# Preparing the last layer's weights inside the first attention, and eight tiles in a written-out order

## The reference

```
x = x + tanh(g_xattn[0]) * attention0(layernorm(x), ctx)   # 32 query heads, 8 kv heads, dim 128, rope, wo
x = x + tanh(g_ffn[0])   * ffn0(layernorm(x))              # weights faked to 4 bits, activations to 8 bits, silu(gate)*up, 512-1376-512
x = x + tanh(g_xattn[1]) * attention1(layernorm(x), ctx)   # channels as tokens: 512 x 512 logits per sequence, q and k from ctx
x = x + tanh(g_ffn[1])   * ffn1(layernorm(x))              # dense 512x512 + bias + 4 LoRA experts of rank 8, softmax router
```

## Time and profile before

| | us |
|---|---|
| median of three runs | 862.97 |
| the profiled execution | 863.2 |
| its span, first to last instruction | 861.2 |
| PE / DVE / ACT / POOL busy in the span | 817.4 / 573.4 / 457.7 / 495.6 |

### The profile page before, as it was taken

One profiled execution on the slowest core, in us unless ns is written; L12 is line 12 of the kernel. 1 busy time (PEld: TensorE's weight loads), 2 busy tenths in 40 slices (PEclk: granted clock), 3 DMA queues, 4 the chain that ended last, 5 costly groups with the idle time before them and its releaser, 6 DMA issues. The chain is left out here.

```text
span 861.2 us, 13801 instructions
## 1 busy us (share of the span) xinstructions
PE 817.4 (95%) x5025; PEld 652.8 (76%) x5025; DVE 573.4 (67%) x1057; ACT 457.7 (53%) x864; POOL 495.6 (58%) x424
## 2 busy tenths in 40 slices
PE   5999999999999999999999999997759999999996
PEld 5778888888888888888888888886526777777774
DVE  4977765656755565565655446446588999999863
ACT  3544555545554444543545434331468878887760
POOL 1767556654566655666457655451247867776750
PEclk9999999999999999999999999999789999999998
DMA  8522132331423313132130130074133333222300
GB/s 258 135 87 80 56 93 59 104 97 38 117 59 87 93 29 93 38 110 70 28 117 25 41 26 2 1 232 133 49 98 75 87 87 98 57 66 64 74 14 25
DMA packets 74499, 66.77 MB, mean 78 GB/s; under 512 B 36112, under 2 KB 53744, under 8 KB 74048
## 3 DMA queue, kind: packets, MB, share of 16 engines
q1 hardware_dynamic: 73472, 65.56, 27.8%
q10 hardware_dynamic: 960, 0.33, 0.1%
HBM read 49.04 MB, written 6.34 MB: 64 GB/s over the span
## 5 line engine op out<-in xcount | busy, mean ns | idle before, releaser
L791 DVE SCALAR_TENSOR_TENSOR x_res<-bank,gate,x_res 128x512 f32<-128x512 f32 x128 | 95.6, 748 | 96.2 <-PE bank L485 95.8
L963 POOL TENSOR_TENSOR prob<-prob,row_inv 128x512 f32<-128x512 f32 x32 | 33.4, 1044 | 191.4 <-DVE row_inv L787 191.4
L949 POOL TENSOR_TENSOR rope_swap<-rope_swap,trig 128x512 f32<-128x512 f32 x80 | 103.9, 1299 | 33.7 <-ACT rope_swap L609 33.6
L78 PE MATMUL bank<-xnT_hi,wq_hi 128*128 128x512 f32 (+1 forms) x264 | 105.4, 399 | 0.7 <-DVE xnT_lo L726 0.7
L480 PE MATMUL bank<-wo_hi,oT_hi 128*128 128x512 f32 x256 | 101.3, 396 | 3.8 <-DVE x_res L791 1.4
L80 PE MATMUL bank<-xnT_hi,wq_lo 128*128 128x512 f32 (+1 forms) x264 | 103.0, 390 | 0.0
L79 PE MATMUL bank<-xnT_lo,wq_hi 128*128 128x512 f32 (+1 forms) x264 | 102.4, 388 | 0.0
L481 PE MATMUL bank<-wo_lo,oT_hi 128*128 128x512 f32 x256 | 101.1, 395 | 0.0
L762 DVE TENSOR_TENSOR rope_cos<-bank,trig 128x512 f32<-128x512 f32 x80 | 54.6, 682 | 69.3 <-PE bank L80 69.3
L608 ACT COPY rope_swap<-bank 64x512 f32<-64x512 f32 x80 | 46.7, 583 | 87.3 <-DVE rope_cos L762 84.4
L1982 POOL TENSOR_TENSOR b_e<-b_e,b_inv 128x512 f32<-128x512 f32 x64 | 69.6, 1091 | 30.2 <-DVE b_inv L1546 29.5
(11 more groups left out here) (228 smaller groups left out, 1960.3 us busy)
## 6 DMA issues: line engine op xcount, KB each, us to landing
wq_raw<-in_L_xattn_wq SPq DMA_DIRECT2D x16, 512.0 KB, 4.1
wo_raw<-in_L_xattn_wo SPq DMA_DIRECT2D x16, 512.0 KB, 3.9
xn<-in_L_ffn_Wd SPq DMA_DIRECT2D x16, 256.0 KB, 3.3
b_ctx<-in_ctx SPq DMA_DIRECT2D x32, 128.0 KB, 2.6
b_k_twice<-b_qk_hi SPq DMA_DIRECT2D x32, 128.0 KB, 2.3
w_T_dram<-w_out SPq DMA_DIRECT2D x28, 128.0 KB, 2.3
w_T<-w_T_dram SPq DMA_DIRECT2D x2, 1376.0 KB, 7.0
xn<-in_L_ffn_Wg SPq DMA_DIRECT2D x10, 256.0 KB, 3.9
```

Of the source, the lines that this page charges most:

```text
L78: pe.matmul(out, a_hi, b_hi, start=first, stop=False)
L791: dve.scalar_tensor_tensor(out=K.x[:, t, :], in0=wo_ps[t % 2][:, :], scalar=K.gate[:, 0:1], in1=K.x[:, t, :], op0=ALU.mult, op1=ALU.add).t ...
L949: pool.tensor_tensor(out=sw, in0=sw, in1=sin_b, op=ALU.mult).then_inc(s_rope, 1)
```

## The change

**Moved into slots 30 and 31 of the attention part:** the selection of experts (DVE, in slot 30 between the first and second, and the second and third accumulate), two `iota` and two `memset` (POOL, at the start of slot 30), `qkv_T` and `base_T(0)` (PE, end of slot 30), `base_T(1)`, `base_T(2)` (slot 31, ahead of the product with v), `base_T(3)` and `b_T` ahead of the last output, `low_T` in the middle of it, `low_b_select` and the first tile's `x_transpose` behind it; with them the copies on ACT, differences on DVE, the statistics of the first four tiles and the first tile's `front`, `x_shifted`, `x_int` and `xT_copy`.

**Loads:** W_base is loaded as soon as the last wq piece is split, the other raw weights ahead of the quantised FFN weights; lora_B comes in 4 DMAs of 128x16x8 elements instead of 16 of 128x4x8; the first tile's context is loaded before the attention part ends.

**Moved between engines, for every tile:** `normalise` of attention1's input goes from DVE to ACT (with a new small `shift_of` on DVE), `x3_lo` from DVE to POOL. `route_end` loses one DVE operation (alpha and z in one). `low` has 132 columns instead of 36.

**Order:** the loops over `it` are replaced on all engines by lists of calls, with explicit waits. Buffers are laid over those of the attention part that are already free.

```diff
+            for par in range(2):
+                sp.wait_ge(s_wq_lo[par], NQP * HKV)
+            load_base(sp, R1, K.a)
             sp.wait_ge(s_proj, NI * (HKV - 1) + pos_of(HKV - 1, "v", 1) + 1)
+            load_block1(sp, K.W1, R1, K.a)
             for w in range(2):
                 sp.dma_start(K.W.T[w][:, :, :], K.T_dram[w]).then_inc(K.s_w_in, 16)
...
-            load_block1(sp, K.W1, K.raw1, K.a)
...
-            load_base(sp, K.raw1, K.a)
+            sp.wait_ge(s_wo, UT * (2 * NPAIR - 2))
+            for par in range(2):
+                load_context(sp, M, ctx_dram, 0, par)
...
+                if U == 2 * NPAIR - 1:
+                    base_T(1)
+                    base_T(2)
...
+                if U == 2 * NPAIR - 2:
+                    qkv_T()
+                    base_T(0)
 
             run_slots(slot)
-            output(2 * NPAIR - 1)
+            base_T(3)
+            b_T()
+            output(2 * NPAIR - 1, low_T)
+            low_b_select()
+            first_x_transpose()
...
+            def selection_of_experts():
+                dve.wait_ge(R1.s_in, 16 * R1.n_loads)
+                dve.wait_ge(s_zero, 2)
+                dve.tensor_copy(M.act_f[:, :], R1.act_i[:, :]).then_inc(s_sel, 1)
+                dve.tensor_copy(M.rank_f[:, :], M.rank_i[:, :]).then_inc(s_sel, 1)
...
                         accumulate(T, T % NT)
+                    if U == 2 * NPAIR - 1:
+                        statistics(k)
+                    if U == 2 * NPAIR - 2 and k == 0:
+                        selection_of_experts()
+                    if U == 2 * NPAIR - 2 and k == 1:
+                        selection_matrices()
...
+            base_low_part(2)
+            last = UT * (2 * NPAIR - 1)
+            accumulate(last, UT)
+            dve.wait_ge(s_x_stat, 2 * UT + 2)
+            front_tile(dve, K, M, 0)
+            accumulate(last + 1, UT + 1)
+            base_low_part(3)
+            for tl in range(2, UT):
+                accumulate(last + tl, UT + tl)
+            low_b_lo()
...
+                    if U == 2 * NPAIR - 2:
+                        pool.iota(M.rank_i[:, :], pattern=[[1, RANK]], base=0, channel_multiplier=0).then_inc(s_zero, 1)
+                        pool.iota(M.part_i[:, :], pattern=[[0, 1]], base=0, channel_multiplier=1).then_inc(s_zero, 1)
...
-    for e in range(E_ALL):
-        load(R.b[:, :, e * RANK:(e + 1) * RANK], a["L1_ffn_lora_B"][e].rearrange("(c p) r -> p c r", p=P))
+    for c in range(DC):
+        load(R.b[:, c, :].rearrange("p (e r) -> p e r", e=E_ALL),
+             a["L1_ffn_lora_B"][:, c * P:(c + 1) * P, :].rearrange("e p r -> p e r"))
...
-            for it in range(NT + 4):
-                if ok(it - 3):
-                    attend_pair(it - 3, 0)
...
+            gate_mm(0, 0)
+            up_mm(0, 0)
+            qk(0, 0)
+            pe.wait_ge(s_gate, 1)
+            gate_mm(0, 1)
```

More of the change, by code:

```diff
@@ new lines, in _ @@
+            logits(2, 2)
+            pe.wait_ge(s_xT_sb, 4)
+            v_item(1)
+            low(0)
+            weights_T(1, 6)
+            pe.wait_ge(s_gate, 10)
+            gate_mm(3, 1)
+            pe.wait_ge(s_v, 2)
+            qk(3, 1)
+            logits(2, 3)
+            weights_T(1, 7)
+            logits(2, 4)
+            pe.wait_ge(s_gate, 11)
+            gate_mm(3, 2)
+            pe.wait_ge(s_up, 10)
+            up_mm(3, 1)
+            attend_pair(1, 0)
+            weights_T(2, 0)
@@ new lines, in _ @@
+            weights_T(3, 5)
+            x3_T(2)
+            pe.wait_ge(s_hTa_sb, 5)
+            down(4)
+            weights_T(3, 6)
+            pe.wait_ge(s_qk_lo[1], 6)
+            v_item(3)
+            logits(4, 2)
+            pe.wait_ge(s_up, 17)
+            up_mm(5, 2)
+            logits(4, 3)
+            low(2)
+            weights_T(3, 7)
+            pe.wait_ge(s_v, 4)
+            x_transpose(6)
+            pe.wait_ge(s_out, 5)
+            gate_mm(5, 2)
+            attend_pair(3, 0)
@@ new lines, in _ @@
+            h_scales(0)
+            scale_gate(1, 0)
+            row_max(0, 4)
+            scale_up(1, 0)
+            reciprocal(0, 1)
+            lo_qk(1, 0)
+            scale_gate(1, 1)
+            row_max(0, 5)
+            row_max(0, 6)
+            make_h(1, 0)
+            scale_up(1, 1)
+            reciprocal(0, 2)
+            front(2)
+            scale_gate(1, 2)
+            row_max(0, 7)
+            scale_up(1, 2)
+            make_h(1, 1)
+            lo_qk(2, 0)
+            output(0)
@@ new lines, in _ @@
+            rest_of_weights()
+            row_max(1, 0)
+            reciprocal(0, 3)
+            statistics(0)
+            scale_gate(2, 0)
+            lo_qk(2, 1)
+            shift_of(0)
+            row_max(1, 1)
+            make_h(1, 2)
+            row_max(1, 2)
+            reciprocal(1, 0)
+            h_scales(1)
+            row_max(1, 3)
+            scale_up(2, 0)
+            front(3)
+            reciprocal(1, 1)
+            scale_gate(2, 1)
+            row_max(1, 4)
+            residual(0)
@@ new lines, in _ @@
+            make_h(2, 0)
+            x3_normalise(0)
+            row_max(1, 5)
+            lo_qk(3, 0)
+            output(1)
+            row_max(1, 6)
+            scale_up(2, 1)
+            reciprocal(1, 2)
+            scale_gate(2, 2)
+            statistics(1)
+            scale_up(2, 2)
+            row_max(1, 7)
+            row_max(2, 0)
+            shift_of(1)
+            make_h(2, 1)
+            reciprocal(1, 3)
+            scale_gate(3, 0)
+            row_max(2, 1)
+            make_h(2, 2)
@@ new lines, in _ @@
+            output(2)
+            row_max(2, 6)
+            make_h(3, 1)
+            row_max(2, 7)
+            scale_gate(4, 0)
+            statistics(2)
+            lo_qk(4, 0)
+            scale_up(4, 0)
+            shift_of(2)
+            zT_lo(0)
+            row_max(3, 0)
+            reciprocal(2, 3)
+            make_h(3, 2)
+            row_max(3, 1)
+            lo_qk(4, 1)
+            h_scales(3)
+            scale_gate(4, 1)
+            reciprocal(3, 0)
+            residual(1)
@@ new lines, in _ @@
+            scale_gate(5, 0)
+            reciprocal(3, 2)
+            lo_qk(5, 0)
+            zT_lo(1)
+            residual(2)
+            statistics(3)
+            scale_up(5, 0)
+            scale_gate(5, 1)
+            x3_normalise(2)
+            finish(1)
+            shift_of(3)
+            reciprocal(3, 3)
+            row_max(4, 0)
+            row_max(4, 1)
+            lo_qk(5, 1)
+            scale_up(5, 1)
+            front(6)
+            reciprocal(4, 0)
+            output(4)
@@ new lines, in _ @@
+            make_h(5, 0)
+            row_max(4, 2)
+            row_max(4, 3)
+            statistics(4)
+            scale_gate(5, 2)
+            route(2)
+            make_h(5, 1)
+            scale_up(5, 2)
+            reciprocal(4, 1)
+            row_max(4, 4)
+            shift_of(4)
+            route_end(2)
+            row_max(4, 5)
+            front(7)
+            scale_gate(6, 0)
+            reciprocal(4, 2)
+            row_max(4, 6)
+            lo_qk(6, 1)
+            row_max(4, 7)
@@ L1756, in _ @@
+            finish(6)
+            route(7)
+            route_end(7)
+            zT_lo(7)
+            finish(7)
         @block.scalar
```

1860 lines of the change are left out of this document (1304 added, 556 removed).

## The result

| | before | after |
|---|---|---|
| median, us | 863.12 (862.83 to 864.4, 4 runs) | 852.25 (849.12 to 856.15, 4 runs) |
| ratio, 95% interval | | 0.9873 (0.9831 to 0.9916) |
| profiled execution / its span | 863.2 / 861.2 | 856.15 / 854.3 |
| measured again, the kernel before beside it | 862.02 (17 runs) | 850.54 (847.73 to 856.11, 6 runs), ratio 0.9870 (0.9840 to 0.9900) |

The change makes the kernel faster by 1.3%, some 11 us. The forecast was 848.0, range 835 to 861. The profiled execution of the kernel after is the slowest of its four; of the repetition there is a profile of the fastest (847.73, span 845.8). The two together tell what varies.

The account below looks back on a forecast made before the run. Tail taken as bound by latency at start and end, by DVE with PE close behind in the middle; from 863.2, -2.2 - 5.9 - 2.6 - 1.0 - 3.0 - 0.3 = -15.0 gives 848.2, forecast 848, range 835 to 861.

Parts of the forecast that it names:

- B: Rival: weight preparation not hidden, lora_B late, clock low through the last output, no steady gain; 857 us, chance 0.19.
- C: Rival: slower, x3_lo waits at the head of POOL's list and delays weigh and product every tile; 866 us, chance 0.08.
- A: Rival: relief worth more, 1.0 us a tile for seven tiles, end gives 5, clock stays up; 839 us, chance 0.28.
- Preparation out of the tail, -9.5: Between last output and first gate: weight preparation moves ahead, so gate_mm could start at 608.1 instead of 617.6, -9.5 us.
- The selection's stall, +4.3: Slot 30: second accumulate waits for the selection, which waits for POOL's iotas; PE stands still 4.3 us, delaying what follows.
- The clock, +3: Attention's end: the new pause puts PE at 1.2 GHz for some 4 us, +2; low_T before 512-column matmuls, +1 (0 to 3).
- wrong if the first gate lies before 611: Sign against the forecast: a first gate matmul before 611 would mean there was no stall.
- First gate to first `weights_T`, 18.5: Start of the tail: first weights_T 18.5 us after the start instead of 27.8, first logits at 11; net -5.9 us.
- DVE relief, -2.6 and -1.0: Middle tiles: work off DVE gives 0.5 us for six tiles less 0.1 for low, -2.6; two base_lo gone, -1.0.
- The end, -3.3: Last 64 us: written-out lists draw later logits forward, -3 (0 to -5); last chain loses one small operation, -0.3.

Follow-up runs that it names:

- e5: Changed kernel with the selection of experts moved behind all four accumulates of slot 30, iotas left in place: 844.35 us, ratio 0.9793 to the kernel before.
- e1: Changed kernel with the two iotas moved among GpSimd's first operations of the program: 847.87 us, ratio 0.9831 to the kernel before.
- e10: e5 plus the first tile's memsets and context splits in the attention part and its qk ahead of the gate: 844.28 us, ratio 0.9793 to the kernel before.
- e11: e10 plus low_T cut in four between the token tiles of the last output: 843.93 us, ratio 0.9794 to the kernel before.
- e7: Kernel before, loops kept, with only x3_lo moved to GpSimd and attention1's normalise to ScalarE: 861.72 us, ratio 0.9987 to the kernel before.
- e6: The changed kernel unaltered, run again as reference: 850.54 us, ratio 0.9870 to the kernel before; its profile is of the fastest execution, 847.73.
- e9: Kernel before with each qk's first product issued three times, more work on TensorE alone: 864.84 us, ratio 1.0028 to the kernel before.

## Why the prediction was right, and where its steps were off

The median is 4 us above the forecast and inside the forecast's own range of 843 to 853. B and C ask for a middle that gains nothing or loses, which the four tiles exclude even without the 0.9 us of moved work. A asked for 1.0 us a tile, a gain of 5 at the end and no fall of the clock behind the stall: the middle gave 0.8 by the marks and 0.6 without the moved work, and the clock fell.

1. *Preparation out of the tail, -9.5: right.* e5 has the stall removed and the rest in place. Its first gate comes 32.50 us after output(29); the step's 608.1 minus 576.41 is 31.7.
2. *The selection's stall, +4.3: right in mechanism, pause a little shorter.* 3.54 us, because the first half of the selection took 0.8 us and not 1.4. The lora_B load cost nothing: VectorE waited for the iota alone. Its four DMAs took 4.7 us to issue, between the 2.0 and the 14.2 of the prediction.
3. *The clock, +3: right in mechanism and, in six profiles of seven, in size.* The first gate lay 39.0 us behind output(29) by the prediction, 39.3 to 39.9 in six profiles and 42.86 in the first. Which of them a launch gets is chance. The sign "wrong if the first gate lies before 611" didn't come. The Trainium skill's rule ("TensorE: Matmul & The Clock Gate", section "HAM oscillation — how this bites in real kernels") held for this pause: in all seven profiles with the pause of 3.5 us, and in e1 with 2.4, the clock fell right behind it, and in e5, e10 and e11 without the pause it stood at 1.00 there. It isn't the only occasion: e7, without the pause, had a fall from 597 to 600, behind two short ones of 0.68 and 1.17 us, which stand in the kernel before as well and there left the clock at 1.00.
4. *First gate to first `weights_T`, 18.5: right.* 18.15 in the first profile, 18.93 in e6; first logits after 10.6 and 10.8 (forecast 11).
5. *DVE relief, -2.6 and -1.0: the mechanism was the step's weak part.* (Its own sum, six tiles at 0.5 less 0.1, is -2.4.) The step took VectorE's busy time for the pace of the tile and thought of the order as neutral there. The four combinations over four tiles are: old order 105.11, old order with x3_lo and normalise moved 105.14, new order without them 104.48, new order with them 101.91. In the old order, at the places tried, the moves gave nothing; in the new one they gave 2.6 us. What the order gives alone can't be read from this: its 0.6 is less than the 0.9 us of moved work, and the new order has the shorter `route_end` and the wider `low` in it as well, which no run took apart. Forecast were 0.4 us a tile; measured are 0.8 by the marks, about 0.6 without the moved work. VectorE's busy time fell to 24.5 us a tile, not to 23: `shift_of`, put at 0.2 to 0.4, took 0.82 us on average, and x3n grew from 0.75 to 0.94. What paces the tile in the old order isn't isolated; e7 and e9 show that VectorE's time and a chain through TensorE and ScalarE lie within 0.2 us of each other there.
6. *The end, -3.3: not confirmed.* From down(6) to the last `attend_pair` 0.4 to 0.7 us were gained, with about 2.6 us more work of TensorE in that stretch, so the marks can't tell whether the step's 3 was too large. The last stretch varies from 17.9 to 21.4 us between profiles with the clock, so its -0.3 can't be checked.

In sum e6 against the execution of before: the first gate comes 2.1 us earlier (forecast 2.2), from there to the last `attend_pair` 10.5 us are gained (forecast 12.5, points 4 to 6 without the last 0.3), and behind it 2.75 (forecast 0.3). So the tail gave 2 us less than forecast, and in e6 the clock, which stayed at 1.00 in the last stretch, gave it back: that e6 comes out at 847.73, next to the forecast's 848.2, is luck by this part. In the first profile the clock was unkind at the start (4.5 us), behind the stall and in the last output (3.6 against e6). The other executions have no profile; that the 4 us between 848 and the median are the missing 2 and the clock is likely from these two and not shown.

## What to carry to other kernels

An engine that is 98% busy and named in nearly every link of the chain need not be what a relief has to aim at, since the next limit can lie just behind it: add a known amount of work to one engine and take some from another, and see what comes through. The same two moves were worth nothing in the old order and 2.6 us over four tiles in the new one; whoever tests them only in the old order throws them away. Marks in a timeline compare two orders only after the work between them has been counted. Work put into a "free" place of another engine's list has to be checked for what stands ahead of its semaphore, for what runs on GpSimd at that moment, and for whether the stall falls where TensorE is fully busy; moving the selection 4 us later in the same list brought 6.6 us (uncertain by some 3 in the medians, 6.8 in the profiles up to the first gate), more than half of the whole change again, and is the version to keep (844.35; the two further edits are not distinguishable from it).

## What the runs showed that I had not expected

- A pause of 3.54 us on TensorE, in the same place of the changed kernel and its variants, was followed by 3.4 us at 1.2 GHz in three executions and by 10.2 in four others (worked out from the windows of 2 us).
- At the program's start the same products of 256 columns stood 0.12 us apart in eight of the fourteen profiles and 0.21 in the other six (before and after differ in this way, and so do two executions of the changed kernel). The eight reach output(29) at 576.2 to 577.2 us, the six at 578.1 to 580.9.
- The last stretch, with the same work, took 17.92 us with the clock at 1.00 in it and up to 21.39 with falls.
- A cast and two tensor_scalar of 4 columns took 1.08 to 1.40 us on VectorE in e1 while GpSimd ran 128x512 operations, and 0.16 to 0.20 in e5 and in the kernel after, where GpSimd had finished. In a list on the critical path, six "free" small operations took 3.7 us in e1.
